# Codes in three parts, two more places for expanded weights, and adjacency loads of 1 MB for the first three chunks

## What is computed

```python
def ggc(x, adj, W, wih, whh, bih, bhh):        # one gated graph convolution
    m = adj @ (x @ W)
    gi, gh = m @ wih.T + bih, x @ whh.T + bhh
    r, z = sigmoid(i_r + h_r), sigmoid(i_z + h_z)
    n = tanh(i_n + r * h_n)
    return (1 - z) * n + z * x

h = relu(ggc(x, adj, ...1)); h = relu(ggc(h, adj, ...2))
x = layernorm(x + h)
support = x @ weight                            # last layer
mask = adj != 0
rank = cumsum(mask, axis=1); deg = rank[:, -1:]; k = minimum(deg, 100)
w = mask * where(rank - (deg - k) > 0, 0.5 ** (k - (rank - (deg - k))), 0)
out = layernorm(x + w @ support + bias)
```

## Time and profile before

| | us |
|---|---|
| median of 3 runs | 365.16 (364.94 to 365.21) |
| the profiled execution, its own time | 365.44 |
| span of its trace, first to last instruction | 363.6 |
| outside the span (365.44 - 363.6) | 1.8 |

### The profile page before, as it was taken

One profiled execution on the slowest core, in us unless ns is written; L12 is line 12 of the kernel. 1 busy time (PEld: TensorE's weight loads), 2 busy tenths in 40 slices (PEclk: granted clock), 3 DMA queues, 4 the chain that ended last, 5 costly groups with the idle time before them and its releaser, 6 DMA issues.

```text
span 363.6 us, 6494 instructions
## 1 busy us (share of the span) xinstructions
PE 337.7 (93%) x2416; PEld 156.3 (43%) x2424; DVE 297.4 (82%) x479; ACT 184.3 (51%) x237; POOL 23.9 (7%) x32
## 2 busy tenths in 40 slices
PE   1998999999999999999999999999899999998972
PEld 1343233333333333333333324453344554887962
DVE  0689889897876976979996577899999999798983
ACT  0202404131041310575295377857796869776992
POOL 2000000000000000000000010202020202102242
PEclk9999999999999999999999999999999999999998
DMA  7999999999999999998889999898969994000011
GB/s 248 413 408 409 408 411 406 410 408 370 409 379 339 399 336 319 326 348 311 287 286 390 402 411 385 298 351 314 387 233 386 359 376 158 16 4 2 2 60 58
DMA packets 32719, 111.08 MB, mean 306 GB/s; under 512 B 3633, under 2 KB 6193, under 8 KB 32689
## 3 DMA queue, kind: packets, MB, share of 16 engines
q1 hardware_dynamic: 31824, 109.20, 79.4%
q10 hardware_dynamic: 864, 1.48, 1.2%
HBM read 109.62 MB, written 1.05 MB: 304 GB/s over the span
## 4 chain that ended last, share of the span: by engine, by line
PE 70%; DMA 9%; DVE 9%; ACT 6%; issue 4%; POOL 1%; POOLq 0%; ACTq 0%; DVEq 0%
PE m_acc L439 37%; PE out L439 15%; DMA stream<-in_adj_t 8%; PE out L544 4%; DVE run L931 3%; PE rz_ps L517 2%; PE rz_ps L503 2%; PE n_ps L544 2%; DVE codes L936 2%; DMA w<-in_w 2%; PE rz_ps L496 2%; PE n_ps L496 2%; PE rz_ps L544 1%; ACT s_in L717 1%; PE m_acc L544 1%
## 5 line engine op out<-in xcount | busy, mean ns | idle before, releaser
L439 PE MATMUL m_acc<-stream,s_in 128*64 128x512 f32 x512 | 125.9, 607 | 3.7 <-issue 2.3
L887 DVE TENSOR_SCALAR codes<-stream 128x1024 uint8<-128x1024 f32 x117 | 76.4, 685 | 4.2 <-DMA stream<-in_adj_t 4.0
L439 PE MATMUL out<-stream,s_mid 128*64 128x512 f32 x272 | 69.1, 595 | 0.8 <-DMA stream<-in_adj_t 0.6
L439 PEld LDWEIGHTS m_acc<-stream,s_in 128*64 128x64 f32 x512 | 33.9, 137 | 66.3 <-issue 53.3
L439 PE MATMUL m_acc<-stream,s_mid 128*64 128x512 f32 x240 | 53.9, 597 | 0.0
L827 POOL TENSOR_TENSOR rstd<-var,mhalf 128x4 f32<-128x4 f32 x16 | 22.0, 1378 | 336.0 <-DVE var L1042 336.0
L936 DVE SCALAR_TENSOR_TENSOR codes<-codes,run 128x1024 uint32<-128x1024 uint32 (+2 forms) x42 | 40.8, 970 | 1.4
L931 DVE TENSOR_TENSOR run<-run,codes 128x2048 uint16<-128x2048 uint16 (+2 forms) x41 | 39.3, 960 | 1.6
L627 ACT ACTIVATE m_high<-m_acc 64x512 f32<-64x512 f32 x13 | 7.7, 595 | 58.8 <-PE m_acc L439 45.7
L717 ACT ACTIVATE wexp<-codes,code_bias 128x2048 uint16<-128x2048 uint8 x18 | 35.7, 1993 | 0.6 <-DVE codes L936 0.5
L439 PEld LDWEIGHTS out<-stream,s_mid 128*64 128x64 f32 x272 | 19.1, 137 | 39.2 <-issue 38.8
(11 more groups left out here) (150 smaller groups left out, 406.0 us busy)
## 6 DMA issues: line engine op xcount, KB each, us to landing
stream<-in_adj_t SPq DMA_DIRECT2D x204, 512.0 KB, 6.1
x_res<-in_x_pairs SPq DMA_DIRECT2D x8, 128.0 KB, 6.6
out_nodes<-stream SPq DMA_DIRECT2D x8, 128.0 KB, 1.9
hx<-in_x_pairs ACTq DMA_DIRECT2D x1, 512.0 KB, 7.4
const<-in_consts ACTq DMA_DIRECT2D x1, 358.0 KB, 6.6
hx<-in_x_pairs ACTq DMA_DIRECT2D x2, 128.0 KB, 6.2
hx<-in_x_pairs ACTq DMA_DIRECT2D x1, 256.0 KB, 8.9
bias_b<-in_bias SPq DMA_DIRECT2D x1, 128.0 KB, 4.9
```

The costliest lines, as they stand in the source:

```text
L439: last = nc.tensor.matmul(to[D * u:D * (u + 1), :], state[:, t * D:(t + 1) * D], stream[:, n % SLOTS, u * CW:(u + 1) * CW], start=start[u] ...
L887: nc.vector.tensor_scalar(edges(p // 2, b, 2 * (p % 2), 2), stream[:, n % SLOTS, :], 0.0, None, ALU.not_equal).then_inc(mask_made, 1)
```

## The change

- **Loads.** adj lies in DRAM in blocks of two pairs, partition by partition: the two pairs of a partition are one row of 8 KB. The loads of pairs 2 to 47 (chunks 0 to 2) bring two pairs each: 23 loads of 1 MB in place of 46 of 512 KB. They use slots 0 to 5; the slot pair is free when both of its pairs are used. Pairs 0 and 1, and all from 48 on, are still loaded alone (4 KB rows, 8 KB apart in DRAM), from 48 on into 7 slots. Both pairs of a large load signal one semaphore.
- **Codes.** The first 12 tiles (before: 10) are cut in three: chunks 0 to 2 in 11 steps in chunks 3 to 5 and one in chunk 6, chunks 3 to 5 in 12 steps in chunks 6 and 7, chunks 6 and 7 afterwards. 20 tiles (before: 22) run over all chunks.
- **Places.** `h` (a half of hx, free after h_made 12) and `k` head the list for REST, so each later block gets a place that was listed two later.
- **Who expands.** VectorE 21 blocks (before 19), ScalarE 43 (before 45). The shares (5,5) and (6,5) come before (7,0).

```diff
+IN_TWOS = 3 * NP
+def slot(n):
+    return n % (SLOTS - 1) if n < IN_TWOS else n % SLOTS
+def in_twos(n):
+    return 2 <= n < IN_TWOS
...
-EARLY = NCH - 2
-CHAIN_EARLY = {6: {10: 1, 11: 1, 12: 1, 13: 1, 14: 1}, 7: {2: 1, 4: 1, 6: 1, 8: 1, 10: 1}}
+PARTS = (slice(0, 3), slice(3, 6), slice(6, NCH))
+GUARD_IN = {3: 0, 6: 1}
+CHAIN_EARLY = ({3: (11, 13, 15), 4: (4, 7, 10, 13), 5: (4, 7, 10, 14), 6: (4,)},
+               {6: (10, 11, 12, 13, 14, 14), 7: (2, 4, 6, 8, 10, 12)})
...
-PLACES = ["w0", "w1"] + [f"s{i}" for i in range(SLOTS)] + ["m"] + [f"d{i}" for i in range(1, 10)]
+PLACES = ["h", "k", "w0", "w1"] + [f"s{i}" for i in range(SLOTS)] + ["m"] + [f"d{i}" for i in range(1, 10)]
...
-CHAIN = [chain_tiles(*x) for x in ((0, 4), (4, 9), (9, 14), (14, 19), (19, 23), (23, 27), (27, 31),
+CHAIN = [chain_tiles(*x) for x in ((0, 5), (5, 10), (10, 15), (15, 19), (19, 23), (23, 27), (27, 31),
                                    (31, 32), (32, 32))]
-CHAIN_CUT = [(1, 2), (2, 4)] + [(1, 2)] * (NCH - 1)
+CHAIN_CUT = [(1, 2), (2, 4), (2, 3)] + [(1, 2)] * 4 + [(0, 1)] * 2
...
+                if both:
+                    sp.dma_start(stream[:, slot(n):slot(n) + 2, :], adj_t[ch, at // 2])\
+                        .then_inc(adj_in[SIGNAL[n]], 16)
+                else:
+                    sp.dma_start(stream[:, slot(n), :], adj_t[ch, at // 2, :, at % 2, :])\
+                        .then_inc(adj_in[SIGNAL[n]], 16)
```

More of the change, by code:

```diff
@@ L83 @@
 BIAS_AT = 5
+IN_TWOS = 3 * NP
[3 more added lines that the diff above has]
+    return 2 <= n < IN_TWOS
+SLOT_HAD = [max([m for m in range(n) if slot(m) == slot(n)], default=None) for n in range(len(LOADS))]
+SIGNAL = [slot(n - n % 2) if in_twos(n) else slot(n) for n in range(len(LOADS))]
+ARRIVED = [sum(SIGNAL[m] == SIGNAL[n] and not (in_twos(m) and m % 2) for m in range(n + 1))
+           for n in range(len(LOADS))]
 COMBINE = (0, 0, 0, 0, 0, 0, 0, 0)
@@ L153, in place_free @@
     return max(before) + 1 if before else 0
[L157 removed]
+PLACE_USED = {f"s{i}": 1 + max(n for n in range(len(LOADS)) if slot(n) == i)
               for i in range(SLOTS)}
@@ L312, in weights @@
                 return s_in[:, NT * D // 2:].bitcast(BF16)
+            if place == "h":
+                return hx[:, N // 4:N // 2].bitcast(BF16)
             if place == "k":
@@ L403, in _ @@
                 for q in range(NP):
-                    load(b * NP + q)
+                    if not (in_twos(b * NP + q) and q % 2):
+                        load(b * NP + q)
                     if b == BIAS_AT - 1 and q == NP - 1:
@@ L910, in fold_sums, with guard, chain @@
                         .then_inc(sum_made, 1)
-            def guard(late):
-                dve.wait_ge(start_made, NCH if late else EARLY)
-                at = run[0][:, EARLY * CW:] if late else run[0][:, 0:EARLY * CW]
-                nc.vector.tensor_scalar(at.bitcast(U16), at.bitcast(U16), float(GUARD * 257),
-                                        None, ALU.add).then_inc(guarded, 1)
-            def chain(j, k, late=True):
-                c, n, i = NCH - 1 - j, tile_step(j, k), codes_count(j, k, late)
-                to = slice(0, NCH) if KT * j + KT - 1 - k >= N_EARLY else \
-                    slice(EARLY, NCH) if late else slice(0, EARLY)
+            def guard(part):
+                chunks = PARTS[part]
+                dve.wait_ge(start_made, chunks.stop)
+                at = run[0][:, chunks.start * CW:chunks.stop * CW].bitcast(U16)
+                nc.vector.tensor_scalar(at, at, float(GUARD * 257), None, ALU.add)\
+                    .then_inc(guarded, 1)
+            def chain(j, k, part=2):
+                c, n, i = NCH - 1 - j, tile_step(j, k), codes_count(j, k, part)
+                to = PARTS[part] if KT * j + KT - 1 - k < N_EARLY else slice(0, NCH)
                 if n == 0:
-                    dve.wait_ge(guarded, 2 if late else 1)
+                    dve.wait_ge(guarded, part + 1)
                 if i > 1:
@@ L1015, in _ @@
                             keep_add(b - 1)
-                    if b == EARLY and q == GUARD_AT:
-                        guard(False)
-                    if b in CHAIN_EARLY and q in CHAIN_EARLY[b]:
-                        for _ in range(CHAIN_EARLY[b][q]):
-                            chain(*chain_tiles(early, early + 1)[0], False)
-                            early += 1
+                    if b in GUARD_IN and q == GUARD_AT:
+                        guard(GUARD_IN[b])
+                    for part, steps in enumerate(CHAIN_EARLY):
+                        for _ in range(steps.get(b, ()).count(q)):
+                            chain(*chain_tiles(early[part], early[part] + 1)[0], part)
+                            early[part] += 1
                     if b == 1 and q == 9:
@@ L1089, in _ @@
             new_h(NCH - 1)
-            guard(True)
+            guard(2)
             for j, k in CHAIN[0]:
```

61 lines of the change are left out of this document (34 added, 27 removed), and 2 rows, old and new, of the table ORDER.

## The result

The changed kernel takes **371.3 us** (median of 6 runs, 370.08 to 376.87) against 365.19 us for the kernel before beside it (6 runs, 364.85 to 365.83). The ratio is 1.0165, with a 95% interval of 1.013 to 1.02 (the run of 376.87 is over 1.5% above the fastest and is left out of the ratio): slower, where 357.6 us (355.5 to 361.5) was forecast. The profiled execution took 371.35 us.

The account below looks back on a forecast made before the run. TensorE was taken as the main engine throughout, with DMA bounding only up to load 44, near 67 us. Terms: -8.9 stands, +0.3 loads, +0.9 new waits, +0.1 tail, sum -7.6; forecast 357.6 us (355.5 to 361.5).

Parts of the forecast that it names:

- The gaps of the loads: Chunks 0 to 2: some large loads issued too late to keep the DMA full, 0.9 us, between 0 and 2.
- The sum of the loads: Large loads up to pair 44: -1.9 for faster rows, +1.3 for pair 44, +0.9 gaps, +0.3 us (-0.9 to +1.8).
- Rows of 8 KB: Large loads: 0.31 us per 8 KB packet, 0.09 us less per 1 MB, 1.9 us over 21 loads.
- rival B: Large loads: 8 KB rows move as two of 4 KB, the 1.9 us fall away, 359.5 us; chance 0.2.
- Pair 44 waits for pair 45: Last large load bounding the kernel: pair 44 must wait until pair 45 lands, +1.28 us.
- Codes in chunks 3 to 5: Eleven new VectorE steps there fit by a hair before mx: 0, at worst 1 us.
- Middle and end: From 240 us on: stands gone -8.9, new waits +0.9, tail +0.1 us.
- ten stands: TensorE's stands from 240 us on, behind VectorE and ScalarE: 7.5 us plus 1.4 for breaks, 8.9 us, all gone.
- the new waits: Second layer: 0.6 us at the node of step 7, 0.3 at the next (0 to 1.2 for both).
- C: Rival: the end is bound by the supply of VectorE's expansions, 360.6 us; chance 0.12.
- Rival D: Single loads reading rows 8 KB apart take 1.75 us a pair for 1.28; 366.6 us or more; chance 0.06.
- 420 GB/s from 36 to 60 us: Sign in the first part: DMA throughput of 420 GB/s or more if large rows help; 408 or less for B.

Follow-up runs that it names:

- e3_loads: The kernel before with only the change's loads and DRAM layout added: 378.93 us, ratio 1.0359.
- v2_twos_deep: Changed kernel with large loads for pairs 8 to 43 only, ring of 12 slots, and ScalarE's step 7 expansion moved behind the square: 359.55 us.
- e12_two_instructions: Changed kernel with 4 KB rows and each 1 MB load issued as two 512 KB instructions, waited for together: 370.4 us.
- e8_rows4k12: Changed kernel with each pair one block in DRAM (1 MB loads, 4 KB rows) and 12 slots in chunks 0 to 2: 360.27 us.
- e14_blocks12: Changed kernel with 512 KB loads, one block a pair, and 12 slots in chunks 0 to 2, each freed by itself: 360.05 us.
- e1_codes: Changed kernel with the loads and layout of before (512 KB, 7 slots); codes, places and expansions as changed: 358.89 us, ratio 0.9815.
- e2_layout: Changed kernel with 512 KB loads in 7 slots as before, but keeping the new layout (4 KB rows 8 KB apart): 364.5 us.
- e6_hybrid6: Changed kernel with chunks 3 to 7 stored as before, one block a pair; 1 MB loads in 6 slots kept: 371.24 us.
- e9_hybrid8: Changed kernel with chunks 3 to 7 stored as before and 8 slots in chunks 0 to 2: 363.97 us.
- e7_hybrid12: Changed kernel with chunks 3 to 7 stored as before and 12 slots in chunks 0 to 2: 361.16 us, ratio 0.9875.

## Why the prediction was wrong, point by point

1. **The gaps of the loads** ("I take 0.9 us of gaps, between 0 and 2") are the step that failed: they are some 11 us. The sum of the loads was +0.3 us and is +13.2 (e3_loads) or +12.4 (371.3 less 358.9). Under it lies one estimate: a load lands 1.6 us after the length of its transfer, 1 us of it ahead of the data, from a store of 128 KB late in the program, where little else was under way. That makes 4.1 us for 1 MB. The load issued at 39.05 took 4.8, but in the rounds it was 6.9 us on average, with the last of the 16 signals up to 2.6 us behind the others. With the rounds' own use of 3.4 us, a landing of 4.1 makes 2.5 us for two pairs, just under the 2.57 of the transfer, and 6.9 makes 3.43. The nearer row was in hand: the load of the earlier trace rows issued at 60.35 took 6.48 us to land. A ring with three places for large loads goes round in landing plus use. With 6.48 us, 1.28 more for the second pair and 2.2 us for using two pairs, that is 10.0 us for three loads: 3.3 us for two pairs in place of 2.57. The 6.48 hold time behind other loads, so this is the upper end; but the trace of after has 3.43. I had written the condition ("issued within about 4 us"), but priced it by a guess where a loop of times from rows would have shown that it fails.
2. **Rows of 8 KB**: 0.31 us and 3% were right (420 against 409 GB/s), and rival B falls. The gain was not to be had, though, since TensorE is as near the bound (v2_twos_deep). That the first pair can only be used with the second cost 4.8 us in e12_two_instructions, not the 1.28 of one pair. In a full ring the 1.28 is about right (point 3). The Trainium skill, "Perfetto Trace Analysis", section "DMA Optimizations", says that splitting a transfer may allow some of it to start sooner. These two runs agree with it: the same 512 KB pieces, used one by one, are 4.8 us faster. For batching, the same section has 2 KB made into 4 or 8 KB as its example; the loads of adj here have no rows under 4 KB, and from 4 to 8 KB the traces have 2.7%.
3. **Pair 44 waits for pair 45**, +1.28 us: the size was right, the place another. At the gates of chunk 3 e8_rows4k12 is 1.3 us behind before and e14_blocks12 0.1 ahead, but the same distance stands at the gates of chunk 0 already. It is load 18 there that waits for its partner: TensorE stands 1.90 us for it at 34.98 us in e8_rows4k12, and 0.95 us at 33.61 in the kernel before.
4. **Codes in chunks 3 to 5**, 0: right. In e1_codes the gates of chunks 2 to 7 are within 0.1 us of before's, and in the kernel after the distance of 11.2 to 11.3 us holds over the same chunks.
5. **Middle and end**, -8.9 + 0.9 + 0.1 = -7.9: right in mechanism, 1.3 us too large. e1_codes' span is 6.6 us shorter. All ten stands went (60.00 of 60 us from 240 on), but the new waits are 1.3 us at the gates of step 8 and 0.8 at two nodes, 2.1 in sum for 0.9. The releaser of the first, x1s, was not on my list: ScalarE's square waits behind an expansion of 2.0 us. C did not occur: no share waits for an expansion.
6. **Rival D**, slower by rows 8 KB apart: such rows do cost time (5.6 us in e2_layout), but not by the mechanism named, a lower rate, nor in the place named. I looked for it in chunks 3 to 7, where the change reads such rows, and there it costs nothing (e6_hybrid6). A pair still takes 1.28 us; what grows is the time to land. It was given 0.06 as a matter of rate, and no rival spoke of the time to land. A rival "the loop of three slot pairs is longer than three transfers" was missing, and it was the outcome.

Of the signs named beforehand, 420 GB/s from 36 to 60 us failed (356), and the loads of chunk 3 landed at their usual distance, which spoke against D. The stand before `node` was gone, and no stand stood after 330 us but 0.50 us for h_c.

## What to carry to other kernels

Before a ring of buffers is regrouped, work out its loop: the time from issue to landing, taken from a row of that stream in the stretch in question, plus the use of everything that is freed together, divided by the loads in the ring. It must be below the transfer time of one load, with room to spare; here it was 3.43 us against 2.57, and the DMA engines ran nearly empty in between. The row must be of loads that meet others under way: a lone store's 1.9 us misled here. Larger loads need more bytes in the ring, not the same; and a faster transfer is worth something only where no compute engine is just behind it.

## What was not expected of the hardware

- With two under way, a 1 MB load took 5.8 to 7.7 us to land from 43 to 75 us, where its transfer needs 2.5 us. One of them had fifteen of its sixteen signals after 4.8 us and the last after 7.4. The engines' share fell to 0.12 at 64 us; with three under way (e9_hybrid8) it was 1.00 from 36 to 60 us at 405 GB/s, with five (e7_hybrid12) 1.01 at 421.
- TensorE's granted clock fell to its lower level for 3.4 us behind single stands of 1.57 to 2.73 us in four traces, and did not behind one of 2.80 us in the kernel after.
- Rows of 4 KB that stand 8 KB apart in DRAM are read at the same rate (1.28 us for 512 KB) as long as enough is queued, but a load lands 0.9 us later (6.4 for 5.5 us), and the times spread: 361.92 to 366.27 us over nine runs of e2_layout, 358.47 to 359.14 over four of e1_codes.
- Small inputs on another queue (`w`) land up to 1.7 us later in the kernels that store chunk 0 two pairs by two pairs (9.2 us of waiting for it in e7_hybrid12, 7.5 in e1_codes). Whether the rows of 8 KB or the rows 8 KB apart do it was not separated, but the latter suffice (9.0 in e2_layout).
